# Embedding gathers at their own pace, two in flight, in a recommendation tower on one core

## The reference

```python
e = jnp.stack([tbl_0[ids[:, 0]], ..., tbl_39[ids[:, 39]]], axis=1)   # (512, 40, 64)
viW = jnp.einsum('bpd,pde->bpe', e[:, i_idx, :], W)                  # 780 pairs
z = jnp.einsum('bpe,bpe->bp', viW, e[:, j_idx, :])
h = jnp.concatenate([z, dense_ctx], axis=1)
h = jnp.maximum(h @ W_top1 + b_top1, 0.0)
h = jnp.maximum(h @ W_top2 + b_top2, 0.0)
y = h @ W_top3
```

## Time and profile before

| | us |
|---|---|
| timed, median of 3 (lowest, highest) | 319.71 (319.37, 320.14) |
| span of the profiled execution | 361.1 |
| time around that span | not given by the trace |
| TensorE busy in the span | 324.8 (90%) |
| VectorE busy | 255.2 (71%) |
| GpSimd busy | 206.5 (57%) |
| ScalarE busy | 106.8 (30%) |

### The profile page before, as it was taken

The page is one execution under the profiler, slowest core; times in us unless marked ns, Lnnn a source line. Parts: engine busy times, 40 slices in busy tenths (PEclk is TensorE's granted clock), DMA queues, the critical chain, the costliest instruction groups (busy, mean ns, idle before and its releaser), DMA issues.

```text
span 361.1 us, 4423 instructions
## 1 busy us (share of the span) xinstructions
PE 324.8 (90%) x1700; PEld 115.7 (32%) x1700; DVE 255.2 (71%) x249; ACT 106.8 (30%) x266; POOL 206.5 (57%) x178
## 2 busy tenths in 40 slices
PE   7999739699888949949959999989999999999997
PEld 2444213133222313312312333333333333333455
DVE  5996535586676856945847899999999999990000
ACT  0216000060505551350767653025049000001032
POOL 3887737354735625634654538989987677770000
PEclk9999988899989969987998999999999999999999
DMA  7941212112212272302211346867798766650000
GB/s 170 337 154 51 60 32 66 43 47 73 57 42 53 78 257 92 79 21 52 73 51 42 81 86 147 176 145 158 151 193 172 170 136 118 117 109 9 15 0 0
DMA packets 17772, 35.34 MB, mean 98 GB/s; under 512 B 3924, under 2 KB 4952, under 8 KB 17624
## 3 DMA queue, kind: packets, MB, share of 16 engines
q0 software_dynamic: 7408, 16.26, 23.4%
q1 hardware_dynamic: 7848, 13.96, 12.9%
q10 hardware_dynamic: 2496, 4.84, 3.9%
HBM read 22.86 MB, written 0.00 MB: 63 GB/s over the span
## 4 chain that ended last, share of the span: by engine, by line
PE 59%; DVE 19%; issue 8%; POOL 6%; another core or an unknown queue 6%; DMA 1%; ACT 0%; DVEq 0%; POOLq 0%
PE y_ps L664 33%; PE z_ps L687 15%; DVE prod L558 14%; PE y_ps L697 4%; POOL prod L378 3%; POOL gathered L349 2%; DVE prod L484 2%; PE t_ps L697 2%; PE y_ps L743 1%; PE t_ps L571 1%; POOL prod L374 1%; DMA lane_rows_sb<-lane_rows 1%; DVE zT L494 1%; DVE x_quad L490 1%
## 5 line engine op out<-in xcount | busy, mean ns | idle before, releaser
L664 PE MATMUL y_ps<-x,w 64*128 64x512 f32 x780 | 190.0, 619 | 29.6 <-DVE prod L558 21.9
L349 POOL DMA_INDIRECT gathered<-in_tbl,ids_sb x128 | 131.2, 1025 | 94.6 <-DVE prod L558 55.9
L558 DVE TENSOR_TENSOR prod<-y_ps,x 128x1024 f32<-128x1024 f32 x89 | 103.8, 1216 | 54.8 <-PE y_ps L664 27.5
L664 PEld LDWEIGHTS y_ps<-x,w 64*128 64x128 f32 x780 | 70.6, 189 | 146.6 <-issue 104.0
L558 DVE TENSOR_TENSOR prod<-y_ps,x_quad 128x1024 f32<-128x1024 f32 x96 | 110.6, 1215 | 3.8 <-PE y_ps L664 1.9
L687 PE MATMUL z_ps<-prod,select 128*32 128x512 f32 x596 | 81.7, 652 | 1.2 <-POOL prod L378 1.2
L417 ACT COPY x<-x_fold 32x128 f32<-32x128 f32 x176 | 52.0, 295 | 84.2 <-DVE x_fold L527 70.6
L378 POOL TENSOR_TENSOR prod<-prod 128x1024 f32<-128x1024 f32 x23 | 55.3, 2406 | 0.8
L374 POOL DMA_DIRECT2D prod<-prod x23 | 21.6, 939 | 22.4 <-DVE prod L558 16.3
L687 PEld LDWEIGHTS z_ps<-prod,select 128*32 128x32 f32 x596 | 15.3, 114 | 59.4 <-issue 39.5
L440 ACT COPY x_mix<-x 64x512 f32<-64x512 f32 x40 | 24.7, 616 | 0.7
(11 more groups left out here) (47 smaller groups left out, 84.8 us busy)
## 6 DMA issues: line engine op xcount, KB each, us to landing
w<-w_rows SPq DMA_DIRECT2D x48, 256.0 KB
prod<-prod POOLq DMA_DIRECT2D x23, 512.0 KB, 4.6
gathered<-in_tbl,ids_sb POOLq DMA_INDIRECT x128
w<-w_rows ACTq DMA_DIRECT2D x1, 1792.0 KB
prod<-in_tbl ACTq DMA_DIRECT2D x6, 256.0 KB
prod<-hot_ids SPq DMA_DIRECT2D x4, 256.0 KB, 3.9
prod<-in_tbl ACTq DMA_DIRECT2D x4, 128.0 KB, 3.3
w<-w_rows ACTq DMA_DIRECT2D x1, 512.0 KB
```

What stands on the lines that cost most here:

```text
L349: nc.gpsimd.indirect_dma_start(gathered[:, slot, c, s * DIM:(s + 1) * DIM], None, tables[f][:, :], bass.IndirectOffsetOnAxis(ap=ids_sb[:, ...
L558: nc.vector.tensor_tensor(prod[:, d % PROD_SLOTS, :, :], y_ps[:, d % DUO_SLOTS, :, :], factor, ALU.mult).then_inc(prod_ready, 1)
L664: last = nc.tensor.matmul(y_ps[:, d % DUO_SLOTS, half, :], w[rows, r % W_SLOTS, d % ROUND, :], x[rows, units[half], :], start=True, stop=True)
```

## The change

The first 100 gathers no longer wait for products. Each gather among them waits until the second-last one has landed, for which every slot gets two semaphores in turn (`IN_FLIGHT = 2`), so that its two waiting readers wait for both. The last 28 are let go in rounds 24 to 34 by products as before, in other groups. Rounds 24, 26, 27, 29, 31 and 33 are summed unadded; before it was 29 alone. `FOLDED` begins at 12, so TensorE transposes units 4 to 11. The fold times are reckoned from `gather_due`, 1.1 products a gather from the 14th on.

```diff
-GATHER_LEAD = 2
-FOLD_LEAD = 6
-FOLDED = range(9, 20)
+FOLD_LEAD = 2
+FOLDED = range(12, 20)
 INSIDE = 3
-GATHERED_FIRST = 16
-ROUND_GATHERS = [4] * 24
-LATE_GATHERS = [1, 1, 2, 1, 1, 3, 1, 2, 1, 2, 1]
-UNADDED = [29]
+GATHERED_FREE = 100
+LANDING = 4
+IN_FLIGHT = 2
+LATE_GATHERS = [4, 1, 4, 3, 1, 4, 1, 4, 1, 4, 1]
+UNADDED = [24, 26, 27, 29, 31, 33]
...
-        after = [0] * GATHERED_FIRST
-        for r, count in enumerate(ROUND_GATHERS + LATE_GATHERS):
-            after += [max(ROUND * r - 1, 1)] * count
+        after = [0] * GATHERED_FREE
+        for n, count in enumerate(LATE_GATHERS):
+            after += [ROUND * (self.quad_start[0] + 1 + n) - 1] * count
         self.gather_after = after
+        self.gather_due = [max(n - 13, 0) * 11 // 10 for n in range(GATHERED_FREE)] + [d + LANDING for d in after[GATHERED_FREE:]]
...
-            gathered = self.gather_after[2 * CHUNKS * (u + 1 - HOT_UNITS) - 1] + FOLD_LEAD
+            gathered = self.gather_due[2 * CHUNKS * (u + 1 - HOT_UNITS) - 1] + FOLD_LEAD
...
-        unit_gathered = [sem(f"unit_gathered{s}") for s in range(GATHER_SLOTS)]
+        unit_gathered = [[sem(f"unit_gathered{s}_{n}") for n in range(IN_FLIGHT)] for s in range(GATHER_SLOTS)]
...
                     pool.wait_ge(prod_ready, plan.gather_after[g - first])
+                elif g - first >= IN_FLIGHT:
+                    ahead, landed = divmod(g - IN_FLIGHT, 2 * CHUNKS)
+                    turn = (ahead - HOT_UNITS) // GATHER_SLOTS
+                    pool.wait_ge(unit_gathered[ahead % GATHER_SLOTS][landed % IN_FLIGHT],
+                                 16 * (CHUNKS * turn + landed // IN_FLIGHT + 1))
                 nc.gpsimd.indirect_dma_start(
...
-                ).then_inc(unit_gathered[slot], 16)
+                ).then_inc(unit_gathered[slot][part % IN_FLIGHT], 16)
...
             def fold_unit(u):
-                dve.wait_ge(unit_gathered[u % GATHER_SLOTS], 16 * 2 * CHUNKS * turn)
+                for landed in unit_gathered[u % GATHER_SLOTS]:
+                    dve.wait_ge(landed, 16 * CHUNKS * turn)
...
-                pe.wait_ge(unit_gathered[u % GATHER_SLOTS], 16 * 2 * CHUNKS * turn)
+                for landed in unit_gathered[u % GATHER_SLOTS]:
+                    pe.wait_ge(landed, 16 * CHUNKS * turn)
```

More of the change, by code:

```diff
@@ L115, in gather_times @@
         parts = 2 * CHUNKS
-        after = [0] * GATHERED_FIRST
-        for r, count in enumerate(ROUND_GATHERS + LATE_GATHERS):
-            after += [max(ROUND * r - 1, 1)] * count
-        assert len(ROUND_GATHERS) == self.quad_start[0] + 1 and len(after) == parts * (UNITS - HOT_UNITS)
+        after = [0] * GATHERED_FREE
+        for n, count in enumerate(LATE_GATHERS):
+            after += [ROUND * (self.quad_start[0] + 1 + n) - 1] * count
+        assert len(after) == parts * (UNITS - HOT_UNITS)
         self.gather_after = after
[L121 to L124, removed]
+        self.gather_due = [max(n - 13, 0) * 11 // 10 for n in range(GATHERED_FREE)] + [d + LANDING for d in after[GATHERED_FREE:]]
+        for u in range(FOLDED.start, UNITS):
+            assert self.transposed_at(u) < ROUND * self.first_round(u) + ROUND
     def mixed(self, u):
```

## The result

| | before | after |
|---|---|---|
| timed, median of 4 (lowest, highest), us | 319.54 (319.13, 320.14) | 346.28 (343.35, 351.15) |
| ratio | | 1.0749, 95% interval 1.0719 to 1.0779 |
| span of the profiled execution, us | 361.1 | 341.5 |
| its own time, us | not given | 343.35 |

The change costs some 24 us where 8.8 were forecast: right in sign, and outside the range of 318 to 334.

The account below looks back on a forecast made before the run. From 205 us on TensorE has no gaps and VectorE is full too; TensorE's time counts one for one. 319.7 + 3.1 (unadded) + 1.8 (transposes) + 1.95 (start) + 2.0 (catching up) = 328.5 us; own range 325.5 to 331.5, wider range 318 to 334.

Parts of the forecast that it names:

- The holes, worth 0 to the timed runs: TensorE's gaps and half clock before 205 us, 46.0 us of the profiled span; removal worth 0 to 4.6 us, value 0.
- the holes are real: Rival: a deep gather queue stalls TensorE and VectorE every fourth round, two in flight ends it; 308 us, chance 0.15.
- Six rounds unadded, +3.1: Five more unadded rounds from 24 on: TensorE +0.85 us each, +4.25, less its 1.16 us wait for GpSimd; +3.1.
- Three transposes, +1.8: Units 9 to 11 by TensorE: three more transposes at 0.59 us on an engine without slack; +1.8.
- worth 0: Units 9 to 11: removing three VectorE folds and most of ScalarE's copies gains nothing, since neither engine is full there.
- The start, +1.95: Early gathers beside tables and weights: the eighth lands at 29.0, TensorE wants it for unit 4 at 27.08; +1.95 us.
- The pace, 1.25 to 1.3: Gathers two in flight: landing 2.0 to 2.5 us after issue, so the wait is all but free; 1.25 to 1.3 us each.
- a slow stream: Rival: each landing takes 3 us rather than 2.1, pace 1.5, waits before units 6 to 12; 336.5 us, chance 0.12.
- Catching up, +2.0: After the late start, gathers for units 6 and 7 land late, together 0.6 to 2.7 us, value +2.0; then the stream gets ahead.
- if the gathers pace at 1.5: Sign that the forecast is wrong: gathers at 1.5 us each rather than a steady 1.25 to 1.3.

Follow-up runs that it names:

- unit 15: The kernel before with unit 15 folded at product 92 in place of 84 (unit 16 moves from 92 to 96): 330.36 us, ratio 1.0354.
- the second profile of before: The kernel before, unchanged, profiled once more: 319.04 us, span 317.2.
- mixtures first: The kernel after, with ScalarE saving the mixture of units 12 to 15 before the quad copies of unit 15: 344.58 us, ratio 1.0773.

## Why the prediction was right and wrong

The runs first: 10.9 (unit 15) + 3.7 (unadded) + 2.0 (transposes) + 8.7 (two in flight) = 25.3, against 24.1 between the times (343.6 - 319.5), 23.9 by the ratio (0.0749 x 319.5) and 24.3 between the spans. Of the 15.3 us that the forecast of 8.8 lacks, the traces place 8.9 at unit 15, 3.7 at the start (5.7 for 1.95) and 2.4 in catching up (4.4 for 2.0).

*The holes, worth 0 to the timed runs.* Right, and shown: the second profile of before has none. The inference from span against time held, and the rival "the holes are real" is dead. Its 317.2 is also within 2.1 of the 315.1 worked out for a span without holes.

*Six rounds unadded, +3.1.* Right: 3.7 alone by the ratio, 3.0 in that run's trace without its late start, 3.4 in the trace of the kernel after from round 25 on. The other groups of late gathers were never run alone; 3.4 leaves them a few tenths at most. Of the reasoning one reading is off, without effect: three gathers stand only in round 29, which was not added before either, so the added rounds had one or two. *Three transposes, +1.8.* Right: 2.0 alone.

*Moved folds.* **This is the step that failed.** The sum has no term for the new fold times. The prediction settled the change of units with "worth 0", counting VectorE's and ScalarE's busy time; ScalarE was idle two thirds of the time. It never asked when a moved fold's copies are done against when they are read, and so put the moved folds at nothing without a reason. The new position stood in the plan: the fold of unit 15 at 92, one product ahead of its first reader at 93. Priced from rows at hand: 4.90 us of copies behind a fold one product, about 1.2 us, ahead of its reader gives a wait of about 3.7 us at once (3.49 measured); the quad copies and the mixtures come behind, and VectorE waits 6.34 more. Idle share of an engine says nothing of latency. It cost 8.9 us in the changed kernel and 10.9 alone, more than the whole forecast of 8.8. The forecast also passed over the loosened assertion, whose only use is to allow such a position.

*The start, +1.95.* The mechanism was right (the eighth gather late for unit 4, TensorE standing before it), the size was not: first product at 34.82 against 29.14, +5.7. The first gather released its waiter 7.60 us after issue, at 12.65, where 11.7 was reckoned; the fifth went at 18.56 for 16.3, into the same long issue (5.11), and unit 4 was there at 30.78 rather than 29. Then came a part that had no term: after the wait of 3.73 the 16 matmuls behind it took 3.39 us instead of 1.92, the granted clock there (seventh number) being 0.57:

```profile
31.00:35.00 4.00, 4.00 (x22) 1.61 (x22) 0.00 (x0) 0.07 (x1) 2.73 (x3) 0.57 0.13 25
```

*The pace, 1.25 to 1.3.* Mis-sized: 1.47. The forecast timed a landing by the end of the data traffic, 1.6 to 1.9 us, and allowed up to 2.5 for its completion. The release comes at 2.40 to 2.44 and the issue 0.26 later, which is over 2.50 on quiet rings already, and a weight load passing adds to it (a release at 3.57 for the gather of 40.58 in the chain, with one 256 KB load of `w` issued beside it, and 5.66 beside `w1`). The pace of 1.47 was the rival "a slow stream", weighed at 0.12. The Trainium skill (DMA: Bandwidth & Descriptors, Anatomy of one DMA — SWDGE (gpsimd) path) has a fixed cost of about 2.0 us. Added to the 0.94 us of issue it gives an estimate of 1.47 a gather, which the trace agrees with as a mean, though its quiet pairs take 2.68 and the rest is load.

*Catching up, +2.0.* Mis-sized with the pace: units 6, 7 and 11 have waits of 1.30, 1.11 and 1.56, where the prediction expected the stream to be ahead by unit 11; up to round 23 there are 11.9 - 5.7 - 1.8 = 4.4 us beside start and transposes.

*What would make it wrong* was partly named: "if the gathers pace at 1.5". The signs for the folds were not among them. With the slow stream's 8 us the forecast would have said 336.5, still 7.1 too low. That sum has 12.0 for start and stream where 10.1 (5.7 + 4.4) were measured, and nothing for the 8.9 of unit 15.

## What to carry to other kernels

When an order or due time is recomputed, list each moved producer with its first reader, and price the latency of the whole hand-over between them (fold, copies, what the copier does next); an idle engine doesn't make it free. A limit on transfers in flight must exceed release time plus next issue over issue time: here 2.66 / 1.25 is above 2, and a limit of four costs nothing where two cost 8.7 us. Where a profiled span is longer than the timed runs by much, profile again before reading it.

## What the runs showed of the hardware

One kernel gave spans of 361.1 and 317.2 us, with the timed runs at 319.5: 46 us of holes belonged to one profiled execution. Starts differ too: in two of the profiled executions a table came 2.5 to 2.9 us late for VectorE, and the first product stood at 31.51 and 31.86 instead of 29.14. With two gathers in flight the times spread (343.35 to 351.15) and with four they do not (334.71 to 335.05), but without any limit they spread as well (334.69 to 339.52), so the spread is not shown to come from the limit.

A wait can cost more than itself. Of the 8.9 us that unit 15 costs in the kernel after, and of the 11.2 without a limit, 6.2 are TensorE's two waits; much of the rest is matmuls at the lower of TensorE's two levels (1.2 GHz) behind them, 12 in 5.49 us where 2.85 is usual; without a limit the granted clock is 0.50 from 173 to 177 us. It need not cost more: with mixtures first the wait for unit 4 was 3.67 us, and the 16 matmuls behind it took 1.92, as without a wait, where behind 3.73 in the kernel after they took 3.39. That is 1.5 us between two executions with the same wait.
